# Vector's loop closed in front of the squared norms, and the row maxima split on POOL

## The reference

```
# layer 0, attention: every head's q and k divided by their length
n = jnp.sqrt(jnp.sum(t * t, axis=-1, keepdims=True)); t / jnp.maximum(n, EPS)
...
# layer 1, attention: 16 heads of 8 features, scaled scores, masked, softmax over keys
att = jnp.where(mask, -jnp.inf, q @ k.T * SCALE)
att = softmax(att); out = att @ v
```

## Time and profile before

| | us |
|---|---|
| runs before, median of 3 | 1853.49 (1850.83 to 1856.77) |
| the profiled execution | 1856.61 |
| its span | 1854.6 |
| PE busy | 1527.7 (82%) |
| Vector busy | 1219.1 (66%) |
| ACT busy | 859.3 (46%) |
| POOL busy | 518.1 (28%) |

### The profile page before, as it was taken

One profiled execution on the slowest core, in us unless ns is written; L12 is line 12 of the kernel. 1 busy time (PEld: TensorE's weight loads), 2 busy tenths in 40 slices (PEclk: granted clock), 3 DMA queues, 4 the chain that ended last, 5 costly groups with the idle time before them and its releaser, 6 DMA issues.

```text
span 1854.6 us, 33561 instructions
## 1 busy us (share of the span) xinstructions
PE 1527.7 (82%) x10072; PEld 921.9 (50%) x10072; DVE 1219.1 (66%) x3591; ACT 859.3 (46%) x1787; POOL 518.1 (28%) x498
## 2 busy tenths in 40 slices
PE   2889999899999999999989898999999811356774
PEld 2455656464655555555555464656554311335553
DVE  5577878686878686877777786868766368811110
ACT  1436464645555554546464646464653512423331
POOL 1322222131313131312222222213130020048886
PEclk7879999999999999999999999999998755578898
DMA  2031221303030303031211212120303000044443
GB/s 72 1 80 40 49 63 30 77 16 86 7 86 12 80 16 83 24 69 39 53 51 41 55 37 55 37 75 18 80 8 86 8 12 1 1 78 94 96 85 58
DMA packets 83239, 90.71 MB, mean 49 GB/s; under 512 B 19520, under 2 KB 73024, under 8 KB 78528
## 3 DMA queue, kind: packets, MB, share of 16 engines
q1 hardware_dynamic: 71872, 80.76, 17.6%
q0 software_dynamic: 11264, 8.92, 3.6%
HBM read 58.95 MB, written 29.92 MB: 48 GB/s over the span
## 4 chain that ended last, share of the span: by engine, by line
PE 50%; issue 16%; DVE 16%; POOL 8%; DMA 3%; ACT 3%; SPq 1%; DVEq 1%; POOLq 0%; ACTq 0%
PE fa L681 7%; PE ba L587 6%; PE bo L840 6%; PE fa L673 6%; PE ba L582 5%; PE ba L593 4%; POOL out L552 4%; PE fa L691 4%; PE facc L691 2%; DVE passed L1497 2%; POOL got L522 2%; DVE nm L1265 2%; DMA QT<-nmT 2%; SPq L341 1%; PE fa L633 1%
## 5 line engine op out<-in xcount | busy, mean ns | idle before, releaser
L1020 ACT ACTIVATE probs<-ba 128x512 f32<-128x512 f32 x640 | 350.0, 600 | 179.2 <-PE ba L593 177.0
L458 POOL TENSOR_TENSOR x<-x,gd 128x512 f32<-128x512 f32 x144 | 182.4, 1267 | 612.5 <-ACT gd L998 596.0
L582 PE MATMUL ba<-QT,KT 75*128 75x512 bf16 (+3 forms) x1024 | 236.4, 309 | 26.4 <-ACT probs L1020 13.7
L587 PE MATMUL ba<-KT,QT 72*128 72x512 bf16 (+3 forms) x1024 | 230.8, 306 | 7.3 <-DVE nm L1265 3.4
L840 PE MATMUL bo<-probs,vp 128*32 128x512 f32 (+3 forms) x2048 | 193.1, 467 | 27.0 <-DVE ao L1278 26.0
L1265 DVE TENSOR_REDUCE nm<-ba 128x1 f32<-128x512 f32 x256 | 174.9, 683 | 33.2 <-PE ba L593 33.1
L582 PEld LDWEIGHTS ba<-QT,KT 75*128 75x128 bf16 x1024 | 87.9, 101 | 184.8 <-ACT probs L1020 99.5
L681 PE MATMUL fa<-f_nT,w 128*128 128x512 f32 x320 | 170.5, 614 | 3.4 <-DVE hh L1257 3.1
L673 PE MATMUL fa<-f_nT,w 128*128 128x512 f32 x320 | 169.7, 612 | 0.0
L593 PE MATMUL ba<-mask_k,identb 128*128 128x256 bf16 (+1 forms) x640 | 164.8, 258 | 0.0
L593 PE MATMUL ba<-mask_q,identb 128*128 128x256 bf16 (+1 forms) x640 | 164.0, 256 | 0.0
(11 more groups left out here) (279 smaller groups left out, 2679.3 us busy)
## 6 DMA issues: line engine op xcount, KB each, us to landing
QT<-qk_parts SPq DMA_DIRECT2D x96, 192.0 KB
KT<-qk_parts SPq DMA_DIRECT2D x96, 192.0 KB
qk_parts<-qkp SPq DMA_DIRECT2D x32, 384.0 KB, 2.5
fc<-in_L_ffn_fc_weight SPq DMA_DIRECT2D x32, 256.0 KB
xin<-in_L_attn_x SPq DMA_DIRECT2D x16, 256.0 KB, 7.4
qk_parts<-qkp SPq DMA_DIRECT2D x16, 256.0 KB, 2.7
out<-x SPq DMA_DIRECT2D x16, 256.0 KB, 2.3
xn_rows<-row SPq DMA_DIRECT2D x16, 256.0 KB, 7.8
```

Source lines behind the costliest of these rows:

```text
L458: pool.tensor_tensor(x1[:], x1[:], gd[:, e % 2], ALU.add).then_inc(S["s_x1g"], 1)
L582: pe.matmul(bank[:, col:col + w], lhsT=KT[0:K_ROWS, head, blk * P:(blk + 1) * P], rhs=QT[0:K_ROWS, head, blk * P:], start=first_, stop=False)
L587: pe.matmul(bank[:, col:col + w], lhsT=QT[0:QK_ROWS, head, blk * P:(blk + 1) * P], rhs=KT[0:QK_ROWS, head, 0:w], start=first_, stop=False)
L1020: act.activation(probs[:, pair % 3, f_], ba[n % 3][:], ACT.Exp, scale=SCALE).then_inc(S["s_exp"], 1)
```

## The change

Two edits. Vector's y phase is split at another place: the first half now ends with `f_bias(1)`, and everything from `f_l2` on is in the second half, so the loop's jump back stands between them. The order of Vector's work within a batch stays as it was. And `max_parts` is removed from Vector and written for POOL, all four steps in one go: half 0 ahead of `add_gated(f, 4)`, half 1 behind the last `add_gated`. Each step waits for the one ahead of it.

```diff
--- before.py
+++ after.py
@@ -457,8 +457,27 @@
                 pool.wait_ge(S["s_x1g"], ADDED * f + e)
                 pool.tensor_tensor(x1[:], x1[:], gd[:, e % 2], ALU.add).then_inc(S["s_x1g"], 1)
 
+            def max_parts(b, half):
+
+                heads = slice(half * HEADS // 2, (half + 1) * HEADS // 2)
+                done = 6 * b + 3 * half
+                pool.wait_ge(S["s_red"], FILLS * b + (half + 1) * FILLS // 2)
+                apart(pool)
+                pool.tensor_copy(nmp[:, half, :, 0], nm[:, :, heads]).then_inc(S["s_mstep"], 1)
+                pool.wait_ge(S["s_mstep"], done + 1)
+                apart(pool)
+                pool.tensor_tensor(nmr[:, :, heads], nm[:, :, heads], nmp[:, half, :, 0], ALU.subtract).then_inc(S["s_mstep"], 1)
+                pool.wait_ge(S["s_mstep"], done + 2)
+                apart(pool)
+                pool.tensor_copy(nmp[:, half, :, 1], nmr[:, :, heads]).then_inc(S["s_mstep"], 1)
+                pool.wait_ge(S["s_mstep"], done + 3)
+                apart(pool)
+                pool.tensor_tensor(nmp[:, half, :, 2], nmr[:, :, heads], nmp[:, half, :, 1], ALU.subtract).then_inc(S["s_nmp"], 1)
+
             def x_phase(f, b, t, g):
                 for e in range(U0):
+                    if b is not None and e == 6:
+                        max_parts(b, 0)
                     if g is not None and e == 3:
                         power(f_rs[:, 0:Q], f_ve[:, 0:Q], "s_varf", "s_rsf", 2 * g + 1)
                     if g is not None and e == 5:
@@ -471,6 +490,8 @@
                         add_gated(f, e - 2)
                 if f is not None:
                     add_gated(f, E0)
+                if b is not None:
+                    max_parts(b, 1)
 
             def y_phase(b, f, r, t):
                 if r is not None:
@@ -1138,7 +1159,7 @@
                     dve.wait_ge(self.sem, self.b * self.per + self.n)
                     apart(dve)
 
-            fc, mc, rc, tc = Steps("s_fc", 59), Steps("s_mstep", 6), Steps("s_rstep", 8), Steps("s_tc", 11)
+            fc, rc, tc = Steps("s_fc", 59), Steps("s_rstep", 8), Steps("s_tc", 11)
 
             def stats(step, x, st, mv):
 
@@ -1316,24 +1337,7 @@
 
 
             def x_phase(f, b, t, g):
-                def max_parts(half, step):
-
-                    heads = slice(half * HEADS // 2, (half + 1) * HEADS // 2)
-                    if step == 0:
-                        dve.wait_ge(S["s_red"], FILLS * b + (half + 1) * FILLS // 2)
-                        mc(dve.tensor_copy(nmp[:, half, :, 0], nm[:, :, heads]), False)
-                    elif step == 1:
-                        mc.last()
-                        mc(dve.tensor_tensor(nmr[:, :, heads], nm[:, :, heads], nmp[:, half, :, 0], ALU.subtract), False)
-                    elif step == 2:
-                        mc.last()
-                        mc(dve.tensor_copy(nmp[:, half, :, 1], nmr[:, :, heads]), False)
-                    else:
-                        mc.last()
-                        dve.tensor_tensor(nmp[:, half, :, 2], nmr[:, :, heads], nmp[:, half, :, 1], ALU.subtract).then_inc(S["s_nmp"], 1)
-
                 if b is not None:
-                    mc.start(b)
                     for n in range(first):
                         maxima(b, n)
                 if t is not None:
@@ -1350,11 +1354,6 @@
                     if b is not None:
                         for n in fills_of[e]:
                             maxima(b, n)
-                        if 5 <= e < 9:
-                            max_parts(0, e - 5)
-                if b is not None:
-                    for step in range(4):
-                        max_parts(1, step)
                 if f is not None:
                     dve.wait_ge(S["s_ym"], U0 * f + U0)
                     dve.wait_ge(S["s_x1g"], ADDED * f + ADDED)
@@ -1400,22 +1399,13 @@
                     if t is not None:
                         step(t)
 
-                if rest:
-                    fc.b = f
-                    if_b(norm, 1)
-                    if_f(f_x1)
-                    if_b(outputs, 2)
-                    if_t(t_logits)
-                    if_b(norm, 2)
-                    if_f(f_logits)
-                    if_f(f_gates)
-                    if_f(f_rank)
-                    if_b(outputs, 3)
+                if not rest:
+                    if_r(r_norm)
+                    if_f(f_bias, 0)
+                    if_r(r_center)
+                    if_f(f_bias, 1)
                     return
-                if_r(r_norm)
-                if_f(f_bias, 0)
-                if_r(r_center)
-                if_f(f_bias, 1)
+                fc.b = f
                 if_f(f_l2)
                 if_r(r_rest, 0)
                 if_f(f_scale)
@@ -1427,6 +1417,15 @@
                 if_t(t_square)
                 if_t(t_row)
                 if_b(outputs, 1)
+                if_b(norm, 1)
+                if_f(f_x1)
+                if_b(outputs, 2)
+                if_t(t_logits)
+                if_b(norm, 2)
+                if_f(f_logits)
+                if_f(f_gates)
+                if_f(f_rank)
+                if_b(outputs, 3)
 
             def y_whole(b, f, r, t):
                 y_phase(b, f, r, t)

```

## The result

| | us |
|---|---|
| kernel before, median of 4 beside it | 1855.13 (1850.83 to 1858.32) |
| changed kernel, median of 4 | 1809.62 (1809.24 to 1810.03) |
| ratio | 0.9756, 95% interval 0.9734 to 0.9778 |
| profiled execution's span, before and after | 1854.6 and 1807.4 |

The spans differ by 47.2 us.

The account below looks back on a forecast made before the run. Vector's jump back before rden, 3.63 us per round, was taken as the cost to move. Moving it gave +1.1 us, the parts -4.5: -3.4 us, from 1856.61 to 1853.2 us (1850.1 in median terms); range 1838 to 1862.

Parts of the forecast that it names:

- Price at the old place: Vector's jump back before rden costs 3.63 us per round, 39.9 us in all; moving it away gains that.
- The clock's part: At the old place, Tensor's stand of about 2 us lowers its clock: 1.53 us in 9 of 11 gaps.
- Price at the new place: Jump before the squared norms delays the first norm reduction, and so oT and the Tensor engine, by 2.2 us.
- All three readings: Delay before the first norm reduction: 2.05 us, 3.00 us, or as little as 1.4 us, by when the jump starts.
- Which reading of the start: Jump starts when the last instruction before it is let go (2.05 us late), or when that ends (3.00 us).
- The clock, 1.53 us in 11 rounds: At the new place, Tensor stands 3.1 us for oT, so its clock falls every round, costing 1.53 us each.
- The parts on POOL: Eight small Vector instructions per batch go to POOL; x2 addition starts 0.32 us earlier in 14 batches, -4.5 us.
- within 0.1: Sign of being right: the addition that makes x2 starts within 0.1 us of POOL's end.
- a jump taken up ahead of the queue: Faster rival at the new place: delay only 1.4 us, total -12.2 us, 1841.3 us; chance 0.22.
- a clock spared: Faster rival: waiting for the first qkr breaks up Tensor's stand; 17 us less than forecast, 1833 us; chance 0.08.
- The inference beside the forecast's sum: Jump's price belongs to the loop's length, not its place, so the moved jump still pays; already charged in full.
- The queue of 22 packets: An instruction queue's 22 packets, 0.36 MB, were read as two for each of the 11 gaps.

Follow-up runs that it names:

- the run with six copies: Changed kernel plus six copies per round of the input to an unused array, issued between the two halves' maxima DMAs; 1884.03 us, ratio 1.0153.
- with the hint: Kernel before plus one instruction at the head of Vector's loop naming its jump's target: 1818.97 us, ratio 0.978; added to the changed kernel: 1811.62 us.
- e4: Changed kernel with the loop closed later, between the first remainder qkr and the last two Newton steps; 1859.86 us, ratio 1.0004.

## Why the prediction was wrong, step by step

- **Price at the old place, 3.63 us per round.** Right: the loop edit alone takes 41.8 us by the medians, 39.9 were summed, and every kernel without a gap has rounds of 83.8 to 84.6 us. The clock's part was right too: it falls in 9 of the 11 rounds of the kernel before, and in none of the changed one.
- **Price at the new place, 2.2 us of delay.** This step failed. The measured delay is 0. All three readings, 1.4 to 3.0 us late, were made from a price measured beside loads at a share of 0.82. In quiet it is 3.06 us from the start of the last instruction, not 5.62, and this fits under the wait for the squares. The row that spoke against it was at hand: the 11 gaps scattered from 4.3 to 5.7 us while the wait for `sq` was 2.14 us in each of these rounds. I read the scatter as noise. It is the time that the first packet of instructions waits for the DMA engines, 2.6 to 3.9 us.
- **Which reading of the start.** The first is borne out: the branch is taken at 663.9, 0.1 us behind the end of the projections, 663.75. From there the bare 3.06 us end at 666.81, 0.8 us inside the wait for the squares, and the next pass is seen to start at 666.8. Had the jump taken 5.4 us there as well, it would have ended at 669.3, 1.7 us late. Counted from the end of the bias additions the gap of 2.3 to 2.6 would end at 667.7 to 668.0, behind 667.59, and it would show.
- **The clock, 1.53 us in 11 rounds.** It followed from the delay and went with it. With both at zero the sum is 11 x -3.63 = -39.9, with the parts -44.4, against 45.5 measured. The mechanism was right, as the run with six copies shows; it had nothing to start from. That -44.4 comes so close is in part luck, since the term of the parts was not exact.
- **The parts on POOL, -4.5 us.** Somewhat too large. The x2 addition starts 0.17 us behind POOL's end, not within 0.1, so 0.24 us are gained per round and not 0.32: 3.4 us in 14 batches. The 4.8 us of the run with the parts alone can't tell the two apart. On POOL the four steps take 1.33 us (659.57 to 660.90) where 1.3 was worked out, and the power behind them still waits 1.39 us.
- **The rivals.** None of the faster ones was it: not a jump taken up ahead of the queue (the price itself was smaller), and a clock spared for another reason than the one given. The rival that would have won, a cheaper jump where the DMA engines are idle, was not among them. The inference beside the forecast's sum, that the price belongs to the loop's length and not to its place, did not hold: loops of nearly the same length paid 2.9, 5.4 and 7.3 us, by what the DMA engines did.
- **The queue of 22 packets.** I took q8's 22 packets for two loads per jump. It was a coincidence: q8 shows 22 in every kernel of this study, with the hint too, and none of them falls into the rounds from 300 to 1300 us. The loads of the jump are on q14, as the fall from 81 to 27 shows; in the rounds of the kernel before there are five packets for each jump.

The Trainium skill, Runtime: NRT & Kernel Launch, Instruction fetch mechanics, says that a taken branch out of the window must fetch its target by DMA. The traces agree, with a packet on q14 behind each of the 11 branches; with the hint there is none. It calls crossing into the next block mostly hidden, and e4's second gap, 1.57 us, is a place where it is not. What was missing from my reading stands in the Trainium skill, DMA: Bandwidth & Descriptors, Queues, rings and completion order: the refill runs on a queue row that the kernel's own DMAs don't use, row 14, and each DMA engine takes the rows that have work in turn, packet by packet. By that rule a refill pays for the traffic beside it, and the traces agree: its first packet starts 1.0 to 1.3 us behind the branch in quiet, 2.6 to 3.9 and 5.1 to 6.3 us under load.

## What to carry to other kernels

A long loop (here some 400 Vector instructions) can pay for each jump back a load of instructions that competes with the kernel's own DMAs, so close it where the engine waits anyway and the DMA share is low, or give the hint. Before a price measured at one place is carried to another, compare what shared resources do at both; scatter in a number of an otherwise repeating kernel is a sign that it may hang on one. Look for the jump itself in the trace, from the branch to the next pass: it is there even where no gap shows. And check for a second gap behind the first: the same code, 60 instructions further on, was 31 us faster.

## What the runs showed of the hardware

- The jump back of a loop of some 400 Vector instructions took, from the branch to the first instruction of the next pass, 2.8 to 3.1 us with the DMA engines at a share of 0.01, 4.8 to 6.2 us at 0.8, and 7.0 to 8.1 us at 0.92 or more. The gaps seen were 2.3 to 2.6, 4.3 to 5.7 and 5.5 to 6.7 us.
- Most of the difference stands ahead of the first packet of instructions: at these three shares it started 1.0 to 1.3, 2.6 to 3.9 and 5.1 to 6.3 us behind the branch.
- The branch was taken before the instruction ahead of it had ended, in the changed kernel 1.5 us before. A gap of 2.19 us, all of it the wait for `sq`, was enough to hide the jump.
- In one position of the code a second gap of 1.3 to 1.6 us followed some 16 instructions later, and the next packet of instructions started 1.8 us before its end; with the code moved by 60 instructions it was gone.
- One hint instruction per round removed the gaps and every load of instructions in the rounds, 0.44 MB. It cost 5.86 us once, at the loop's end, in one kernel and 2.7 in another.
- Beside POOL's pass over `qkr` a Newton step of two Vector instructions took 0.72 us and the next one 1.27; without it each took 0.40.
